# A graph network's two scattering passes: gather rings of twelve steps, transposed indices, and a Gram sum moved

## The chip, the cores and the metric

One core of a Trainium2 chip runs the whole program. The metric is the device time of one execution in microseconds; lower is better. Two kernels are compared by runs on the same chip.

## The reference, cut to what matters

50,000 nodes with 256 features, 12,500 edges sorted by destination. Two layers follow each other.

```python
h = relu(layernorm(x))                     # layer 0
deg = 1 + count of each node in dst
scaled = (h @ W + b) * rsqrt(deg)
x = x + (segment_sum(scaled[dst], src) + scaled) * rsqrt(deg)
h = relu(layernorm(x))                     # layer 1
up = h @ W_up ; tpw = mlp(edge_attr_16) ; sh = edge_attr_4
msg = segment_sum(tensor_product(up[src], sh, tpw), dst)
A = msg @ W_lin ; B = polynomial(A) ; o = B @ WB + h @ Wsc
x = x + batch_normalised(o)                # over all nodes
```

## The kernel before, in words

The core works in stages. A preparation counts degrees and makes the edge weights (to about 155 us). The node pass p1 follows: 98 groups of 512 nodes (`G`), each loaded to one of eight slots of `big`, gives x1 and writes it to `x1_tab`. Then come two edge passes over 49 steps (`S`) of 256 edges each, two rows of 128. The first pass, e1 (about 710 to 1058 us), gathers rows of `x`, computes layer 0's message and scatters it, added, into `x1_tab`. The second, e2 (1058 to 1406 us), gathers rows of `x1_tab`, forms layer 1's message and scatters it, added, into `msg_tab`. The pass e3 over the ranked destinations and the final node pass p2 end the program.

Each engine has its own program, and they meet through semaphores. `done(eng, sem, s, d)` waits until step s-d has been signalled; `landed(eng, slots, s, d)` waits for the transfers of step s-d. A step function `run(eng, n, skew, body, first=2, unroll=4)` writes the first steps out, loops over blocks of `unroll` steps and writes the rest out. `run_written_out` writes out every step.

What sets the order around the change is the program of POOL (GpSimd), which issues every indirect transfer:

- While p1 runs, `dst_step` gathers 98 columns of node data (line 495). `list_step` then makes 98 small scatters to `list_tab` (line 516), each waiting for the one before to land, with one more node gather between them. `pace` (line 489) ties both to the groups that p1 has finished, three transfers a group.
- In e1, step s gathers step s (two transfers, `gather`, line 529) and then scatters step s-4 (two transfers, `scatter_add`, line 540). In e2 it scatters step s-5. The gathered rows lie in `xg`, a ring of four steps inside `big`; a gather waits until ScalarE has read the step that used its slot (`relu` of s-4).
- `scatter_add` waits for `add` (ScalarE's copy of the merged rows, line 1132), for `sidx` (VectorE's target rows) and for the landing of the scatter one step earlier:

```python
done(pool, sm["add"], s, d)
done(pool, sm["sidx"], s, d)
landed(pool, out_sems, s, d + 1, dmas=2)
```

- VectorE and ScalarE wait for step s-4's scatter before they refill the ring of four that holds the target rows and the merged rows (lines 1517 and 1128).

On TensorE, `spread_own` (line 853) lays the step's 128 indices along the free axis by a product with the identity, so that VectorE (e1, line 1493) or ScalarE (e2, line 1200) can compare each index with each other one; `turn` (line 862) transposes features, `merge` (line 870) adds up rows of equal index. e1 also carries the 49 odd groups of p1: SyncE loads them from `x1_odd` to `big` slots 0 to 3 (line 665) once all of x1 has landed, VectorE takes their moments two steps later, and TensorE adds their Gram products (`add_group`, line 801) four steps later, between `turn` and `spread_own`.

Of the kernel before, what the change touches and what calls it, by code (L numbers as in the profile page):

```python
# [33 lines left out]
XS = 8  # L34
NOWHERE = 1 << 20
# [115 lines left out]
def build(nc, x, src, dst, ea16, ea4, W, b, Wup0, Wup1, M1, M2, M3, M4, Wlin0, Wlin1, Wsc0, Wsc1,  # L151
          Wc0, Wc1, WB0, WB1, gamma0, beta0, gamma1, out):
    with ExitStack() as ctx:
# [138 lines left out]
        bsb = poly[:, 4 * D:8 * D].rearrange("p (s k e) -> p s k e", s=2, k=4)  # L292
        squares = sb("squares", [P, 2, 2, D])
# [131 lines left out]
        def _(pool):  # L425
# [72 lines left out]
            def dst_step(s):  # L498
                pace(s.k)
                of_node_step(0, s.k)  # L500
# [11 lines left out]
            def list_step(s):  # L512
                t = s.k
                pace(T + 2 * t)
# [3 lines left out]
                pace(T + 2 * t + 1)  # L518
# [4 lines left out]
            def gather(got_sems, s, which, table, free):  # L523
# [3 lines left out]
                for i in range(2):  # L527
                    t = 2 * s.k + i
                    pool.indirect_dma_start(xg[:, s.slot(0, 4), i, :], None, table, rows_of(idx3[:, which, t:t + 1])  # L529
                                            ).then_inc(got_sems[s.slot(0, 4)].sem, 16)  # L530
# [41 lines left out]

            pool.wait_ge(pre["cleared"].sem, CLEARED)
            run_written_out(S, 5, e2_step)


            def e3_step(s):
                if s.live() and s.k >= 4:
                    gather(e3_got, s, 0, x1_tab, e3_free)
# [160 lines left out]
        def _(pe):  # L740
# [107 lines left out]
            def spread_own(sm, s):  # L848
# [3 lines left out]
                for i in range(2):  # L852
                    last = mm(spread[s.slot(0, 2)][:, i * P:(i + 1) * P],   # L853
# [952 lines left out]
```

## Time and profile before

| | |
|---|---|
| median of three runs | 2046.6 us (2044.68 to 2050.34) |
| the profiled execution's own time | 2046.1 us |
| its span in the trace | 2043.9 us |
| busy share: TensorE, VectorE, ScalarE, POOL | 85%, 84%, 75%, 58% |
| e1, first gather to last landing | about 710 to 1058 us |
| e2 | about 1058 to 1406 us |

All times in the rows are microseconds from the start of the span, and a mean of one is in nanoseconds. A line `L529` is line 529 of the kernel. In a timeline the brackets at the end tell how long the engine sat idle before the instruction and what ended that; "issue" is time in which it waited for nothing that the profile shows. The program's names in a row are those of the memory that is touched: `xg` and the rows of `big` are both `big`, and most small tiles lie in `o_rows`. The chain of waits is followed backwards from the last instruction, step by step, to what released it. POOL is busy here only while it issues a transfer; the transfer itself goes on beside it.

### The profile page before, as it was taken

To read this page: it belongs to the slowest core of one execution; us is meant where nothing else is said; L and a number is where in the kernel's file an instruction comes from. 1 tells how busy PE (TensorE), PEld (TensorE's weight loads), DVE (VectorE), ACT (ScalarE), POOL (GpSimd) and SP (SyncE) were. 2 spreads that over 40 slices of the span, in tenths; PEclk is the share of its full clock that TensorE was granted. 3 is DMA by queue.
4 is the path that set the end of the run, shared out by engine and by line. 5 is a ranking of instruction groups with operands and counts; after the bars stand their busy time and mean duration, and the time that the engine had idled before them with its cause. 6 is when DMAs were issued, how large, how long until landed. Compare 5 with 4: busy or idle time off the path is not lost.

```text
span 2043.9 us, 53847 instructions
## 1 busy us (share of the span) xinstructions
PE 1728.9 (85%) x14740; PEld 1472.5 (72%) x14740; DVE 1710.5 (84%) x7602; ACT 1536.8 (75%) x3485; POOL 1191.1 (58%) x1166
## 2 busy tenths in 40 slices
PE   4988999999999889888857877775999967778885
PEld 3656888888888767777746666664888857777775
DVE  5777999999999878887838888885888879999885
ACT  3756878878787667877756667664999968889885
POOL 3103754455554567777756777776444229998751
PEclk9999999999999999999979899997999979999998
DMA  4669676666766567777745666667655549999994
GB/s 131 241 237 177 230 245 229 235 237 228 246 231 241 183 161 161 162 155 157 161 80 99 119 122 121 118 116 141 186 177 178 170 158 335 337 341 306 376 363 173
DMA packets 186260, 412.09 MB, mean 202 GB/s; under 512 B 48056, under 2 KB 73788, under 8 KB 186186
## 3 DMA queue, kind: packets, MB, share of 16 engines
q1 hardware_dynamic: 116634, 335.50, 47.3%
q0 software_dynamic: 56448, 74.95, 20.4%
q10 hardware_dynamic: 13104, 0.81, 1.6%
q8 instruction: 28, 0.46, 0.1%
q14 instruction: 46, 0.38, 0.1%
HBM read 207.34 MB, written 206.34 MB: 202 GB/s over the span
## 4 chain that ended last, share of the span: by engine, by line
PE 42%; DVE 13%; issue 12%; DMA 12%; POOL 10%; ACT 8%; SPq 1%; DVEq 1%; ACTq 0%; POOLq 0%
PE bank L842 16%; PE bank L822 5%; DVE st L1389 4%; DMA big<-in_x_dram,idx 4%; POOL big L529 4%; ACT hb L1126 3%; POOL msg_tab L540 3%; PE bank L983 3%; PE bank L801 3%; PE bank L838 3%; DMA big<-x_tab,idx 2%; DMA out_dram<-x1b 2%; PE bank L973 2%; POOL x_tab L540 2%; PE bank L862 2%
## 5 line engine op out<-in xcount | busy, mean ns | idle before, releaser
L1389 DVE BATCH_NORM_STATS2 st<-big 128x6 f32<-128x256 f32 x882 | 314.5, 412 | 82.3 <-DMA big<-x_tab,idx 64.1
L842 PE MATMUL bank<-o_rows,ht 128*128 128x256 f32 x1568 | 372.1, 379 | 0.0
L842 PEld LDWEIGHTS bank<-o_rows,ht 128*128 128x128 f32 x1568 | 298.7, 191 | 49.1
L822 PE MATMUL bank<-ident,hb 128*128 128x128 f32 x1568 | 210.8, 278 | 86.4 <-ACT hb L1126 69.6
L529 POOL DMA_INDIRECT big<-x_tab,idx x196 | 193.5, 987 | 149.4 <-issue 139.8
L495 POOL DMA_INDIRECT o_rows<-node_tab,idx x196 | 188.3, 961 | 137.9 <-issue 55.1
L822 PEld LDWEIGHTS bank<-ident,hb 128*128 128x128 f32 x1568 | 177.3, 142 | 116.4 <-issue 88.9
L1126 ACT ACTIVATE hb<-big,rs 128x256 f32<-128x256 f32 x392 | 216.4, 592 | 10.8 <-DVE rs L1412 10.1
L1087 ACT ACTIVATE hb<-big,rs 128x256 f32<-128x256 f32 x392 | 207.4, 590 | 21.2 <-DVE rs L1412 21.2
L1070 ACT ACTIVATE sd<-mv,eps_col 128x4 f32<-128x4 f32 (+1 forms) x343 | 101.0, 295 | 161.8 <-DVE mv L1398 160.4
L1025 PE MATMUL bank<-fin_w,ht 128*128 128x128 f32 x1568 | 203.3, 276 | 0.0
L1025 PEld LDWEIGHTS bank<-fin_w,ht 128*128 128x128 f32 x1568 | 192.1, 193 | 2.3
L540 POOL DMA_INDIRECT x_tab<-o_rows,sidx x98 | 156.1, 1593 | 59.4 <-ACT o_rows L1132 24.9
L1398 DVE BATCH_NORM_AGGREGATE mv<-st 128x2 f32<-128x6 f32 x1470 | 147.2, 158 | 49.4 <-DVE st L1389 7.5
L540 POOL DMA_INDIRECT msg_tab<-o_rows,sidx x98 | 157.2, 1604 | 53.5 <-issue 26.6
L516 POOL DMA_INDIRECT list_tab<-idx,rank_i x98 | 96.7, 987 | 155.7 <-DMA list_tab<-idx,rank_i 126.4
L1469 DVE SCALAR_TENSOR_TENSOR x1b<-bank,o_rows,big 128x192 f32<-128x192 f32 x392 | 183.7, 469 | 0.0
L853 PE MATMUL bank<-ident,own 128*128 128x128 f32 x392 | 74.2, 315 | 98.9 <-DVE own L1533 95.4
L1098 ACT COPY ht<-bank 128x512 f32<-128x512 f32 x196 | 105.3, 589 | 63.3 <-PE bank L822 63.3
L1421 DVE BATCH_NORM_STATS2 st<-big 128x6 f32<-128x256 f32 x392 | 142.8, 407 | 3.3 <-issue 3.3
L1126 ACT ACTIVATE h<-big,rs 128x256 f32<-128x256 f32 x196 | 108.2, 608 | 44.7 <-DVE rs L1412 44.7
L801 PE MATMUL bank<-o_rows 128*64 128x64 f32 (+1 forms) x3136 | 112.9, 224 | 34.2 <-ACT o_rows L1076 34.2
(267 smaller groups left out, 4486.7 us busy)
## 6 DMA issues: line engine op xcount, KB each, us to landing
big<-in_x_dram SPq DMA_DIRECT2D x97, 512.0 KB, 4.2
x_tab<-x1b SPq DMA_DIRECT2D x97, 512.0 KB
big<-x_tab SPq DMA_DIRECT2D x97, 512.0 KB, 5.8
out_dram<-x1b SPq DMA_DIRECT2D x97, 512.0 KB, 4.3
x_odd<-x1b SPq DMA_DIRECT2D x48, 512.0 KB
big<-x_odd SPq DMA_DIRECT2D x48, 512.0 KB
msg_tab<-zeros SPq DMA_DIRECT2D x50, 256.0 KB, 2.2
tpw_tab<-o_rows SPq DMA_DIRECT2D x49, 256.0 KB, 2.0
```

Of the source, the lines that this page charges most:

```text
L495: pool.indirect_dma_start(node_edge[:, t, i, :], None, node_tab, rows_of(idx3[:, i + 1, t:t + 1])).then_inc(node_in[0].sem, 16)
L529: pool.indirect_dma_start(xg[:, s.slot(0, 4), i, :], None, table, rows_of(idx3[:, which, t:t + 1])).then_inc(got_sems[s.slot(0, 4)].sem, 16)
L540: pool.indirect_dma_start(table, rows_of(sidx[:, s.slot(d, 4), i:i + 1]), addb[:, s.slot(d, 4), i, :], None, compute_op=ALU.add).then_inc( ...
L801: return mm(gram[half:half + C, 0:b.shape[-1]], a, b, start=False, stop=False)
L822: last = nc.tensor.transpose(bank[q][:, (2 * j + k) * P:(2 * j + k + 1) * P], hb[:, s.slot(2, 2), 2 * q + j, k * P:(k + 1) * P], ident[:])
L842: last = mm(y, ht[:, q, (2 * j + k) * P:(2 * j + k + 1) * P], w_sb[:, k, :], start=False, stop=(j == 1 and k == 1))
L1025: last = mm(y, ht[:, 2 * s.slot(3, 2) + q, at], fin_w[:, k, :], start=False, stop=(j == 1 and k == 1))
L1087: return s_act(hb[:, a, j, :], xj(big, s.slot(1, XS), D)[:, j, :], ACT.Relu, bias=rs[:, 0, a, 1, j:j + 1], scale=rs[:, 0, a, 0, j:j + 1])
L1126: return s_act(h, row, ACT.Relu, bias=r[:, 1, j:j + 1], scale=r[:, 0, j:j + 1])
L1389: last = v.bn_stats(st[:, k, j, :], row)
L1398: last = v.bn_aggr(mv[:, k, a, j, :], st[:, k, j, :])
L1469: last = v.scalar_tensor_tensor(out=x1[:, j, C:D].rearrange("p (x c) -> p x c", x=3), in0=y[:, C:D].rearrange("p (x c) -> p x c", x=3), sc ...
```

## The change

The ring of gathered steps becomes twelve deep in both passes. In e1 four steps lie in `f_x` and eight in `big` slots 4 to 7; in e2 eight lie in `big` slots 0 to 3 and four in `f_x`. POOL gathers twelve steps before e1's first scatter (ten before e2's, and one more in step 0) and spreads the remaining ones over the steps by `rows_ahead`. It scatters step s in its step s, so `d` is 0. `dst_step` is tied to four transfers a group instead of three, and the tie of `list_step` begins at group 24 instead of 32 and ends at 88 instead of 97. The loops of VectorE and ScalarE over e1 and e2 have blocks of twelve steps. `spread_own` uses transposes. `add_group` in e1 moves to the end of TensorE's step. e3's first four gathers go into e2's last four steps.

```diff
+RING = 12
@@ build
+        head_rows, tail_rows = (big[:, i:i + 4, :].rearrange("p b (h a d) -> p (b h) a d", h=2, a=2) for i in (0, 4))
+        e1_rows = [f_x[:, i] for i in range(4)] + [tail_rows[:, i] for i in range(8)]
+        e2_rows = [head_rows[:, i] for i in range(8)] + [f_x[:, i] for i in range(4)]
@@ POOL
-            def pace(n):
-                if n % 3 == 0 and n // 3 > 3:
-                    pool.wait_ge(p1["x1"].sem, 2 * (n // 3 - 3))
+            def pace(group):
+                if group > 3:
+                    pool.wait_ge(p1["x1"].sem, 2 * (group - 3))
             def dst_step(s):
-                pace(s.k)
+                if s.k % 4 == 0:
+                    pace(s.k // 4)
             def list_step(s):
-                pace(T + 2 * t)
+                if t % 3 == 0:
+                    pace(T // 4 + 2 * t // 3)
...
-                pace(T + 2 * t + 1)
                 of_node_step(1, t)
...
+            def rows_ahead(k, first, last):
+                return [n for n in range(first, S) if (n - first) * (S - last) // (S - first) == k]
+            def e1_gather(k):
+                s = Step(0, k, k, S, 4)
+                gather(e1_got, s, 1, x, lambda s: done(pool, e1["relu"], s, RING), e1_rows[k % RING])
+            for k in range(4):
+                e1_gather(k)
+            for k in range(4, RING):
+                if k % 2 == 0:
+                    pool.wait_ge(p1["x1"].sem, 2 * (G - 4 + (k - 4) // 2))
+                e1_gather(k)
             def e1_step(s):
-                if s.live():
-                    gather(e1_got, s, 1, x, lambda s: done(pool, e1["relu"], s, 4))
-                if s.k == 4:
+                for k in rows_ahead(s.k, RING, 5):
+                    e1_gather(k)
+                if s.k == 0:
                     x1_landed(pool)
-                scatter_add(e1, e1_out, s, 4, x1_tab)
-            pool.wait_ge(p1["x1"].sem, 2 * (G - 4))
-            run_written_out(S, 4, e1_step)
+                scatter_add(e1, e1_out, s, 0, x1_tab)
+            run_written_out(S, 0, e1_step)
             all_landed(pool, e1_out, S, dmas=2)
+            for k in range(RING - 2):
+                e2_gather(k)
+            pool.wait_ge(pre["cleared"].sem, CLEARED)
             def e2_step(s):
-                if s.live():
-                    gather(e2_got, s, 2, x1_tab, lambda s: done(pool, e2["relu"], s, 4))
-                scatter_add(e2, e2_out, s, 5, msg_tab)
-                if s.k == S:
-                    pool.wait_ge(e3["relu"].sem, e3["relu"].base)
-                    all_landed(pool, e2_got, S, dmas=2)
+                for k in rows_ahead(s.k, RING - 2, 6):
+                    e2_gather(k)
+                if s.k == S - 5:
                     pool.wait_ge(pre["list_in"].sem, 16)
-                if s.k > S:
-                    k = s.k - S - 1
-                    gather(e3_got, Step(0, k, k, S, 4), 0, x1_tab, e3_free)
+                if s.k >= S - 4:
+                    k = s.k - (S - 4)
+                    gather(e3_got, Step(0, k, k, S, 4), 0, x1_tab, e3_free, xg[:, k])
+                scatter_add(e2, e2_out, s, 0, msg_tab)
@@ TensorE, spread_own
-                    last = mm(spread[s.slot(0, 2)][:, i * P:(i + 1) * P], 
-                              own[:, s.slot(0, 2), i:i + 1].to_broadcast([P, P]), ident[:],
-                              start=True, stop=True)
+                    last = nc.tensor.transpose(spread[s.slot(0, 2)][:, i * P:(i + 1) * P],
+                                               own[:, s.slot(0, 2), i:i + 1].to_broadcast([P, P]), ident[:])
@@ TensorE, e1_step: from behind turn() to the end of the step
                 if s.live(4):
                     done(pe, odd["relu2"], s, 4)
                     settle(pe)
                     add_group(h2b[:, (s.slot(4, 2) + S) % 2])
@@ ScalarE and VectorE, e1 and e2 (skews as before)
-            run(act, S, 3, e1_step)
+            run(act, S, 3, e1_step, first=1, unroll=RING)
-            run(dve, S, 3, e1_step)
+            run(dve, S, 3, e1_step, first=1, unroll=RING)
```

Where ScalarE's `relu` and VectorE's `edge_moments` read `xg[:, s.slot(.., 4)]` they now read `e1_rows` or `e2_rows` at slot modulo twelve. `gather`'s own wait, that the gather four steps earlier has landed, stays.

## Rows read from the trace of the kernel before

**Rows 1.** The page, its busy time by engine (us, share, instructions).
```profile
PE 1728.9 (85%) x14740; PEld 1472.5 (72%) x14740; DVE 1710.5 (84%) x7602; ACT 1536.8 (75%) x3485; POOL 1191.1 (58%) x1166
```

**Rows 2.** Busy time in stretches; columns: stretch, us, engines, TensorE clock, DMA share, GB/s.
```profile
740.00:1024.00 284.00, 252.38 (x2439) 215.31 (x2440) 227.21 (x1197) 222.19 (x514) 224.66 (x172) 1.00 0.74 159
1089.00:1367.00 278.00, 208.66 (x1678) 178.07 (x1677) 241.97 (x1133) 188.86 (x420) 218.42 (x169) 0.93 0.64 119
```

**Rows 3.** Chain of waits, mid first pass; columns: start, us, what.
```profile
871.35 0.48 ACT o_rows L1132
...
872.10 0.30 POOL x_tab L540
...
874.02 1.57 POOL x_tab L540
...
875.89 1.01 POOL big L529
...
877.21 4.53 DMA big<-in_x_dram,idx
```

**Rows 4.** Timeline of POOL, first pass: first scatter, tail, first gather of second pass.
```profile
733.16 1.63 POOL L540 DMA_INDIRECT x_tab<-o_rows,sidx  x1 [10.57 <-ACT o_rows L1132]
...
1033.96 1.55 POOL L540 DMA_INDIRECT x_tab<-o_rows,sidx  x1 [0.30 <-issue]
1038.51 1.55 POOL L540 DMA_INDIRECT x_tab<-o_rows,sidx  x1 [3.00 <-DMA x_tab<-o_rows,sidx]
...
1057.89 1.02 POOL L529 DMA_INDIRECT big<-x_tab,idx  x1 [3.18 <-DMA x_tab<-o_rows,sidx]
```

**Rows 5.** Chain of waits, end of the second pass.
```profile
1373.49 0.29 POOL msg_tab L540
...
1375.35 3.81 DMA msg_tab<-o_rows,sidx
...
1379.23 0.71 issue
1379.94 2.17 POOL msg_tab L540
```

**Rows 6.** Timeline of POOL, second pass: last early gather, first and last step's scatter.
```profile
1071.75 0.95 POOL L529 DMA_INDIRECT big<-x_tab,idx  x1 [0.30 <-issue]
1082.18 1.61 POOL L540 DMA_INDIRECT msg_tab<-o_rows,sidx  x1 [9.48 <-ACT o_rows L1132]
...
1400.30 1.62 POOL L540 DMA_INDIRECT msg_tab<-o_rows,sidx  x1 [0.57 <-issue]
```

**Rows 7.** Timeline of all engines where the first pass begins.
```profile
711.23 0.29 DVE L1539 COPY o_rows<-o_rows 128x98 f32<-128x98 f32 x1 [1.01 <-DMA o_rows<-node_tab,idx]
...
715.65 16.48 SPq L665 DMA_DIRECT2D big<-x_odd  x5
715.89 0.75 DVE L1389 BATCH_NORM_STATS2 st<-big 128x6 f32<-128x256 f32 x2 [3.70 <-DMA big<-in_x_dram,idx]
...
721.83 1.40 DVE L1389 BATCH_NORM_STATS2 st<-big 128x6 f32<-128x256 f32 x4
```

**Rows 8.** Timeline of POOL while the list is written: first and last list scatter.
```profile
330.97 1.02 POOL L516 DMA_INDIRECT list_tab<-idx,rank_i  x1 [0.42 <-POOL rank_i L509]
...
707.43 0.99 POOL L516 DMA_INDIRECT list_tab<-idx,rank_i  x1 [1.44 <-DMA list_tab<-idx,rank_i]
```

**Rows 9.** Waits by line between 330 and 708; columns: total us, times, longest.
```profile
POOL list_tab L516 <- DMA list_tab<-idx,rank_i: 126.4, 68, 3.9
```

**Rows 10.** Groups of instructions, 740 to 1024: Gram products, spread, turn.
```profile
L801 PE MATMUL bank<-o_rows 128*64 128x64 f32 (+1 forms) x1370 | 49.4, 224 | 31.6 <-ACT o_rows L1076 31.6
...
L853 PE MATMUL bank<-ident,own 128*128 128x128 f32 x168 | 29.9, 300 | 0.0
...
L862 PE MATMUL bank<-ident,o_rows 128*128 128x128 f32 x172 | 25.7, 272 | 0.0
```

**Rows 11.** Waits by line between 740 and 1024.
```profile
DVE rs L1547 <- issue: 3.0, 9, 0.4
```

More of the change, by code:

```diff
@@ L517, in list_step, with gather @@
                                         ).then_inc(list_out[0].sem, 16)
-                pace(T + 2 * t + 1)
                 of_node_step(1, t)
             run_written_out(T, 0, list_step)
-            def gather(got_sems, s, which, table, free):
+            def gather(got_sems, s, which, table, free, rows):
                 landed(pool, got_sems, s, 4, dmas=2)
@@ L528, in gather @@
                     t = 2 * s.k + i
-                    pool.indirect_dma_start(xg[:, s.slot(0, 4), i, :], None, table, rows_of(idx3[:, which, t:t + 1])
+                    pool.indirect_dma_start(rows[:, i, :], None, table, rows_of(idx3[:, which, t:t + 1])
                                             ).then_inc(got_sems[s.slot(0, 4)].sem, 16)
@@ L554, in _, with e2_gather @@
+            run_written_out(S, 0, e1_step)
             all_landed(pool, e1_out, S, dmas=2)
-            def e2_step(s):
-                if s.live():
-                    gather(e2_got, s, 2, x1_tab, lambda s: done(pool, e2["relu"], s, 4))
-                scatter_add(e2, e2_out, s, 5, msg_tab)
-                if s.k == S:
-                    pool.wait_ge(e3["relu"].sem, e3["relu"].base)
-                    all_landed(pool, e2_got, S, dmas=2)
+            def e2_gather(k):
+                s = Step(0, k, k, S, 4)
+                gather(e2_got, s, 2, x1_tab, lambda s: done(pool, e2["relu"], s, RING), e2_rows[k % RING])
@@ L571, in e3_free @@
                 landed(pool, ex_out, s, 4)
-            pool.wait_ge(pre["cleared"].sem, CLEARED)
-            run_written_out(S, 5, e2_step)
+            run_written_out(S, 0, e2_step)
             def e3_step(s):
                 if s.live() and s.k >= 4:
-                    gather(e3_got, s, 0, x1_tab, e3_free)
+                    gather(e3_got, s, 0, x1_tab, e3_free, xg[:, s.slot(0, 4)])
             run_written_out(S, 0, e3_step)
@@ L879, in e1_step @@
                     turn(hg[:, s.slot(2, 2)], bank[0], e1["turned"])
-                if s.live(4):
-                    done(pe, odd["relu2"], s, 4)
-                    settle(pe)
-                    add_group(h2b[:, (s.slot(4, 2) + S) % 2])
                 if s.live():
@@ L900, in e1_step @@
                     last.then_inc(e1["xw"].sem, 1)
+                if s.live(4):
+                    done(pe, odd["relu2"], s, 4)
+                    settle(pe)
+                    add_group(h2b[:, (s.slot(4, 2) + S) % 2])
             run(pe, S, 4, e1_step)
@@ L1160, in e1_step @@
                     for i in range(2):
-                        last = s_act(hg[:, a, i, :], xg[:, s.slot(1, 4), i, 0:D], ACT.Relu,
+                        last = s_act(hg[:, a, i, :], e1_rows[s.slot(1, RING)][:, i, 0:D], ACT.Relu,
                                      bias=rs[:, 0, a, 1, i:i + 1], scale=rs[:, 0, a, 0, i:i + 1])
@@ L1188, in e2_step @@
                     for i in range(2):
-                        last = relu_row(h2[:, a, i, 1:ROW], xg[:, s.slot(1, 4), i, :], rs[:, 0, a], i)
+                        last = relu_row(h2[:, a, i, 1:ROW], e2_rows[s.slot(1, RING)][:, i, :], rs[:, 0, a], i)
                     last.then_inc(e2["relu"].sem, 1)
@@ L1213, in e2_step @@
                     merged_rows(e2, e2_out, s, 4, bank[7])
-            run(act, S, 4, e2_step)
+            run(act, S, 4, e2_step, first=1, unroll=RING)
             def e3_step(s):
@@ L1522, in scatter_to, with edge_moments @@
                 one.end()
-            def edge_moments(sm, got_sems, s, dmas):
+            def edge_moments(sm, got_sems, s, dmas, rows):
                 landed(dve, got_sems, s, 0, dmas=dmas)
-                return moments(sm, "chain_a", 0, [xg[:, s.slot(0, 4), i, 0:D] for i in range(2)], s)
+                return moments(sm, "chain_a", 0, [rows[:, i, 0:D] for i in range(2)], s)
             def take_own(sm, s, index):
@@ L1641, in e2_step @@
                     one.end()
-            run(dve, S, 3, e2_step)
+            run(dve, S, 3, e2_step, first=1, unroll=RING)
             dve.wait_ge(pre["list_in"].sem, 16)
```

6 lines of the change are left out of this document (3 added, 3 removed).

## The prediction

> **What bounds the kernel now.** The page comes first: TensorE and VectorE are busy 85% and 84% of the span and POOL 58% [rows 1]. That is a mean over stages, so the two edge passes, the only stages that the change rebuilds, are read alone. In the middle of e1 POOL is busy 225 of 284 us, VectorE 227, TensorE 252; in e2 218, 242 and 209 of 278 [rows 2]. None is full.
>
> What sets the pace is seen in the starts of POOL's scatters. From e1's first scatter to the gather that waits for all of them lie 324.73 us for 49 steps, 6.63 each [rows 4]; in e2 318.12 us for 48 spacings, 6.63 again [rows 6]. Two stages with unlike arithmetic have one pace. In e1 the chain of waits runs from a gather's landing (4.53 us) over VectorE and ScalarE to the copy of the merged rows, which ends 0.27 us before the scatter that it releases [rows 3]. That is the wait which the deeper ring removes: the gather of step s+1 stands behind the scatter of step s-4 in POOL's program, and the scatter waits for arithmetic that waits for an earlier gather.
>
> A second wait ends almost with it. `scatter_add` waits until the scatter one step earlier has landed. Where e1 has no more gathers, 4.55 us lie between the second scatter of a step and the first of the next, and the releaser is the transfer [rows 4]. At the end of e2 the same: issue to landing 3.81 us, then 0.71 us until the next scatter [rows 5]. With the 1.86 to 1.92 us between a step's two scatters, a step with nothing else on POOL takes 6.41 (1.86 + 4.55) to 6.45 us (1379.94 less 1373.49) [rows 4, 5]. With gathers in between I find 6.58 as the median of e1's 48 spacings and 6.565 of e2's (first and last steps in rows 4 and 6). POOL's own issuing, with two gathers, is 1.92 + 1.87 + 1.32 + 1.25 = 6.36 us [rows 3, 6]. So the serial landing of scatters bounds both passes, POOL's issuing is 0.1 to 0.2 us below it, and the gather's wait that the ring removes is third.
>
> **The change part by part.**
>
> *The ring in the steady passes.* It takes the gather's wait away and 12 of 49 steps' gathers out of e1's loop, so POOL issues (49 x 3.79 + 37 x 2.57) / 49 = 5.7 us a step. The scatter's wait is unchanged, and it is the one left: late next is the landing. What remains to win is the difference between mean and median spacing, which start, end and single late copies make. e1: 49 x 6.58 = 322.4 against 324.7, -2.3 us. e2: 48 x 6.565 = 315.1 against 318.1, -3.0 us. Bounds: nothing at the present pace, and -0.17 x 97 = -16 us if every step falls to the 6.45 of a step without gathers. I take the medians, since three steps in four still carry gathers.
>
> *Ten gathers ahead of e2's first scatter, an eleventh in step 0.* Before, six steps of gathers end at 1072.7 and POOL idles 9.48 us until the first scatter at 1082.18 [rows 6]. Now 22 transfers come first. The first is at 1057.89 [rows 4]; before, the 12th started at 1071.75 and took 0.95 [rows 6]; ten more at 0.95 + 0.30 bring the 22nd to 1084.25, its end to 1085.2 and the scatter to 1085.5: +3.4 us. The arithmetic does not gain from it, since gathers come every 2.5 us either way. e2 in sum: +0.4 us.
>
> *The start of e1.* VectorE is done with p1 at 710.22. It then waits 1.01 us for node data and 3.70 us for the first gather, whose transfers start only when the list is done [rows 7]. The list now starts earlier: the 98 gathers before it, issued at POOL's 1.25 us each, end near 301 where they now reach 331, for the tie of four a group seldom holds. List scatters stay as they are, (707.43 - 330.97) / 97 = 3.88 us each, 126.4 us of it waits for their own landing [rows 8, 9]; that puts the list's end near 683 and the first eight gathers, 10 us, right behind. So both waits go, 4.7 us. VectorE meets the next one two steps later: the odd group's moments at 721.83 would come at 717.1, but SyncE issues that load only at 715.65, when all x1 has landed [rows 7]. A load of 512 KB at the 2 to 4 us in which e1's smaller transfers land [rows 3, 5] arrives at 717.7 to 719.7. I take 718.3, so -3.5 us on e1's first scatter; the ends are 0 and -4.7. Gathers in p1's last 30 us cost nothing: POOL's DMA work is hidden beside compute in p1, and the list work that they displace made as many transfers. If that cover went, p1 would lose at most the 10 us of eight gathers; nothing before points to it.
>
> *Spreading by transpose.* The two products of a step show as four matmul instructions and 29.9 / 43 = 0.70 us; the four transposes of `turn` take 25.7 / 43 = 0.60 us, so two take 0.30 [rows 10]: 0.40 us off TensorE per step. TensorE is busy 252.4 / 43 = 5.9 of 6.6 us in e1, so this is slack beside the scatters: 0. Only in the first steps, before scatters set the pace, can it show, 4 x 0.4 = 1.6 us, twice that at the low clock, over four steps; I take 0, as VectorE is the one without gaps there.
>
> *The Gram sum at the end.* It lets the spread go ahead of a wait for ScalarE; nothing of it stands on the scatter's path and the first live one comes after the first scatter: 0. ScalarE's next `relu2` waits for it a step later, covered by TensorE's 0.7 us of idle time a step; uncovered, it would cost up to its own 49.4 / 43 = 1.15 us a step [rows 10].
>
> *Loops of twelve.* Nine turns of VectorE's loop show 3.0 us, 0.33 each [rows 11]. Three turns are left. Both lie beside the scatters: 0, with at most +-3 us.
>
> *e3's gathers in e2's last steps* sit as before between scatters; e3 starts from the last scatter's landing: 0.
>
> **Sum:** -3.5 - 2.3 + 0.4 = -5.4 us. Against the profiled execution's 2046.1 us (span 2043.9 and 2.2 around it) that gives 2040.7; the median of the runs, 2046.6, is 0.5 higher, so **2041 us**. A measurement of this kernel can tell about 0.3%, 6 us, from no change, and the forecast is just inside.
>
> **Rivals.**
>
> *The ring frees the pass.* If the landing seen in rows 4 and 5 were itself lengthened by the coupled pattern, POOL's issuing or the arithmetic would bound. At 5.97 us a step (POOL's issuing and a small wait) both passes win 98 x 0.66 = 65 us: 1982 us. For it: e1's chain of waits names gathers. Against it: steps without gathers are no faster than 6.41. Chance 0.06.
>
> *The spacing falls to 6.45.* The landing is shorter when gathers are not in step with scatters. At 6.45 the passes win 16 us instead of 5.3: 2030 us; at 6.50, 2035. For it: steps without gathers run so. Chance 0.22.
>
> *The gathers are not early after all.* The list ends with p1, because it is bound by landings and by the groups. The head gains nothing: 2044.5 us. Chance 0.14.
>
> *TensorE's clock falls in e1 (the slower side).* The spread's product is gone and transposes move as little as they do in e2, where the granted clock is 0.93 against e1's 1.00 [rows 2]; TensorE gets more idle time. Work of 5.9 - 0.4 = 5.5 us a step at 2.4 GHz meets the 6.58 us pace until a fifth of it runs at 1.2 GHz, a granted clock of 0.90; from there each hundredth costs 49 x 0.055 x 2 = 5 us, so at 0.88 the kernel stands at 2051 us. For it: e2's clock. Against it: e2's 0.93 leaves its pace at the same 6.63. Chance 0.08. The Trainium skill, TensorE: Matmul & The Clock Gate, section Part 4: PE-mode transpose, says that transposes do not count as busy time for the clock as products do, which speaks against this part of the change; by that rule this rival would be likelier. The transposes of `turn` in e1, as many instructions as the spread's, stand beside a clock of 1.00, so the trace shows no sign of it at this share.
>
> **Numbers.** Forecast 0.50; its own range 2036 to 2046. The second rival reaches down to 2030 and the fourth up to 2051, so 2031 to 2048 leaves out the first, half of the fourth and the end of the second, about 2 in 10 with the unknown costs. Faster by over 0.3% (below 2040.5): the first two rivals and a third of the forecast, 0.06 + 0.22 + 0.16 = 0.44. Slower by over 0.3%: the clock's case, 0.08. Within: 0.48.
>
> **What would show it.** In the changed profile: scatters still 6.5 to 6.6 us apart, now all with the transfer as releaser; VectorE's wait for gathers gone in both passes and a new wait for `add`'s slots, the scatter four steps back, in its place; e1's first scatter near 729.7; e2's first scatter 27.6 us after its first gather; the list done near 683; e1's clock at 1.00. A spacing under 6.3 us would make the reading of the bound wrong; an e1 start before 728 or after 733 the reading of its head.

## The result, and the profile after

The changed kernel takes 2063.64 us (median of five runs, 2057.11 to 2067.74) where the kernel before took 2046.41 beside it: the ratio is 1.0077 with a 95% interval of 1.0054 to 1.0101. The forecast of 2041 us was wrong, and so was its sign. The profiled execution took 2063.85 us with a span of 2062.1, 18.2 us more than the span before.

Four points on POOL's timeline say where the 18.2 us lie: e1's first scatter, e2's first gather, e2's first scatter, and the first scatter of e2's last step. Timeline of POOL, kernel after (start us, duration us, engine, line, operation, idle time before it and what ended it):

```profile
729.62 1.63 POOL L545 DMA_INDIRECT x_tab<-o_rows,sidx  x1 [3.17 <-ACT o_rows L1154]
...
1052.10 1.55 POOL L545 DMA_INDIRECT x_tab<-o_rows,sidx  x1 [3.05 <-DMA x_tab<-o_rows,sidx]
...
1057.91 1.02 POOL L534 DMA_INDIRECT big<-x_tab,idx  x1 [2.41 <-DMA x_tab<-o_rows,sidx]
...
1087.28 1.73 POOL L545 DMA_INDIRECT msg_tab<-o_rows,sidx  x1 [0.30 <-ACT o_rows L1154]
...
1420.91 1.62 POOL L545 DMA_INDIRECT msg_tab<-o_rows,sidx  x1 [0.54 <-issue]
```

| point | before [rows 4, 6] | after | this stretch adds |
|---|---|---|---|
| e1's first scatter | 733.16 | 729.62 | -3.5 |
| e2's first gather | 1057.89 | 1057.91 | +3.6 |
| e2's first scatter | 1082.18 | 1087.28 | +5.1 |
| last step's scatter of e2 | 1400.30 | 1420.91 | +15.5 |
| end of the span | 2043.9 | 2062.1 | -2.4 |

These are the points of one execution of each kernel. The head wins what was forecast, e1 gives it back, and e2 loses 20.6 us: 5.1 before its first scatter and 15.5 in its 48 spacings, which are now 6.95 us in the mean (median 6.92) where they were 6.63 (6.565). e1's median spacing is unchanged (6.58). The -2.4 us of the later stages has no cause in the change that a run shows: from the last step's scatter to the end of the span the twelve kernels of this document take 635.2 to 645.6 us.

The page's busy line and the two windows of the middle of each pass:

```profile
PE 1726.8 (84%) x14544; PEld 1450.5 (70%) x14544; DVE 1699.0 (82%) x7602; ACT 1538.6 (75%) x3485; POOL 1207.0 (59%) x1166
```

```profile
core 0: us, PE busy (x) PEld busy (x) DVE busy (x) ACT busy (x) POOL busy (x), PEclk, DMA share, GB/s
740.00:1024.00 284.00, 254.97 (x2343) 203.85 (x2341) 220.95 (x1194) 222.82 (x513) 205.26 (x154) 0.98 0.72 153
1089.00:1367.00 278.00, 195.25 (x1515) 163.72 (x1513) 227.54 (x1076) 179.95 (x400) 215.00 (x155) 0.90 0.57 111
```

On the page TensorE and VectorE fall by one and two points against [rows 1], POOL rises by one. Against [rows 2] every engine does less in e2's window: VectorE 227.5 us for 242.0, TensorE 195.3 for 208.7. Nobody became the bound by being full; everyone waits more. POOL falls only by 3 us although it starts fewer transfers (155 for 169): its operations became longer. That is the first hint.

**The start of e1** came at the forecast time. SyncE's odd load is issued at 713.26 (715.65 in [rows 7]) and VectorE waits for it:

```profile
713.26 1.79 SPq L688 DMA_DIRECT2D big<-x_odd  x4
```

```profile
718.21 1.40 DVE L1411 BATCH_NORM_STATS2 st<-big 128x6 f32<-128x256 f32 x4 [2.85 <-DMA big<-x_odd]
```

**e1's spacings** are 6.3 to 6.8 us, most of them 6.5 to 6.6, but for three pairs: 8.29 and 7.55 at scatters 2 and 3, 7.30 and 8.51 around the 23rd step, 7.15 and 8.30 around the 35th. The last two pairs lie 12 steps apart, the length of the new loop. Waits by line in e1's window (engine, what waits, what it waits for: total us, times, longest), then VectorE's timeline at the first of the two:

```profile
DVE sidx L1543 <- DMA x_tab<-o_rows,sidx: 17.7, 27, 1.9
...
DVE rs L1569 <- issue: 10.1, 2, 5.2
```

```profile
856.22 0.16 DVE L1543 TENSOR_TENSOR sidx<-sidx_f,trash 128x2 int32<-128x2 f32 x1 [0.48 <-DMA x_tab<-o_rows,sidx]
861.56 0.18 DVE L1569 RECIPROCAL rs<-sd 128x4 f32<-128x4 f32 x1 [5.18 <-issue]
```

At each turn of the loop VectorE does nothing for 5 us and waits for no other engine. In [rows 11] nine turns cost 3.0 us together, none over 0.4. The DMA view shows what goes on meanwhile. Its queue q14 carries instructions, 8192 bytes a packet (queue: packets, MB, share). First the kernel before and the kernel after, both from 740 to 1024; then after again, in the 0.5 us from 859.5, inside the first idle time:

```profile
q14 instruction: 6, 0.05, 0.0%
...
q14 instruction: 21, 0.17, 0.2%
...
q14 instruction: 1, 0.01, 3.9%
```

That packet starts at 859.56 and VectorE works again at 861.56. At every twelve-step turn of the five kernels that have them (after, b_u12, a_late, a_nott and a_psum, four turns each) exactly one instruction packet starts in the idle time, 1.9 to 2.4 us before VectorE goes on. At the nine turns of the four-step loop in the kernel before there is none in the 4 us before.

**e2's spacings.** Groups of the instructions between 1100 and 1400 (busy us, mean ns of one, idle before them by releaser), before and then after:

```profile
L540 POOL DMA_INDIRECT msg_tab<-o_rows,sidx x91 | 145.8, 1603 | 39.7 <-issue 24.8 <-ACT h L1126 8.2 <-ACT o_rows L1132 3.6
```

```profile
L545 POOL DMA_INDIRECT msg_tab<-o_rows,sidx x86 | 149.0, 1733 | 50.6 <-issue 29.1 <-DVE sidx L1543 13.8 <-ACT o_rows L1154 4.5
L1543 DVE TENSOR_TENSOR sidx<-sidx_f,trash 128x2 int32<-128x2 f32 x44 | 7.0, 160 | 47.9 <-DMA msg_tab<-o_rows,sidx 47.9
```

A scatter is issued in 1733 ns instead of 1603. And VectorE, which in this stretch of the kernel before waited 31.5 us for gathers, now waits 47.9 us for scatters to land, since it may write the indices only when the slot's last user is through. One step on the timeline shows what that does. After, POOL and the DVE rows that matter:

```profile
1251.10 1.57 POOL L545 DMA_INDIRECT msg_tab<-o_rows,sidx  x1 [0.31 <-issue]
...
1254.91 0.16 DVE L1543 TENSOR_TENSOR sidx<-sidx_f,trash 128x2 int32<-128x2 f32 x1 [1.00 <-DMA msg_tab<-o_rows,sidx]
...
1255.61 0.55 DVE L1659 TENSOR_TENSOR big<-big,o_rows 128x384 f32<-128x384 f32 x1
1255.71 1.94 POOL L545 DMA_INDIRECT msg_tab<-o_rows,sidx  x1 [0.45 <-issue]
...
1257.95 1.57 POOL L545 DMA_INDIRECT msg_tab<-o_rows,sidx  x1 [0.30 <-issue]
```

The same place in the kernel before:

```profile
1253.73 0.16 DVE L1521 TENSOR_TENSOR sidx<-sidx_f,trash 128x2 int32<-128x2 f32 x1
...
1254.45 0.55 DVE L1637 TENSOR_TENSOR big<-big,o_rows 128x384 f32<-128x384 f32 x1
1255.58 1.62 POOL L540 DMA_INDIRECT msg_tab<-o_rows,sidx  x1 [0.50 <-issue]
```

Before, the addition of the message's vector part (L1637, 128x384, both inputs in SBUF) has ended 0.58 us before the scatter starts. After, the landing releases both VectorE's indices and POOL's next scatter, so the two engines run in step: the same addition (now L1659) starts 0.10 us ahead of the step's first scatter, and that scatter takes 1.94 us instead of 1.62. So it is, 0.02 to 0.10 us ahead, in 30 of the 43 steps between 1100 and 1400. The 0.32 us come on top of the chain "scatter, scatter, landing, scatter" that sets the pace. In 30 steps they are 9.6 us, and over all 49 steps of e2 the first scatter lasts 1.84 us in the mean where it lasted 1.63, 10.4 us in sum. The rest of the 15.5 us is not read from durations: it lies in single longer spacings, two of them at the loop's turns. The theory is therefore: **two prices that the prediction had at nothing, the turn of a twelve-step loop and the new phase of VectorE against POOL's scatters**. The rivals are that the ring's gathers disturb the landings, that ten steps gathered ahead are the loss, and that TensorE's new parts (spread by transposes, late Gram, lower clock) are.

### The profile page after: what moved, and what is told of

It is laid out like the page before. It is cut to its first block, busy times and chain, and to the rows that moved or that the text cites. A ratio compares the mean times of both kernels' runs of the same rounds, so it can differ in the third digit from the quotient of the medians.

```text
span 2062.1 us, 53155 instructions
## 1 busy us (share of the span) xinstructions
PE 1726.8 (84%) x14544; PEld 1450.5 (70%) x14544; DVE 1699.0 (82%) x7602; ACT 1538.6 (75%) x3485; POOL 1207.0 (59%) x1166
## 4 chain that ended last, share of the span: by engine, by line
PE 42%; issue 14%; DVE 13%; POOL 12%; DMA 9%; ACT 8%; SPq 1%; DVEq 1%; ACTq 0%; POOLq 0%
PE bank L865 16%; DVE st L1411 5%; PE bank L845 5%; POOL msg_tab L545 4%; ACT hb L1148 3%; DMA x_tab<-o_rows,sidx 3%; POOL big L534 3%; PE bank L861 3%; PE bank L1005 3%; DMA out_dram<-x1b 3%; PE bank L824 2%; POOL x_tab L545 2%; PE bank L995 2%; PE bank L1009 2%; DMA msg_tab<-o_rows,sidx 2%
## 5 line engine op out<-in xcount | busy, mean ns | idle before, releaser
L1411 DVE BATCH_NORM_STATS2 st<-big 128x6 f32<-128x256 f32 x816 | 289.0, 409 | 32.5 <-DMA big<-x_tab,idx 29.7
L534 POOL DMA_INDIRECT big<-x_tab,idx x164 | 164.7, 1004 | 139.4 <-issue 129.9
L545 POOL DMA_INDIRECT msg_tab<-o_rows,sidx x98 | 169.0, 1724 | 54.9 <-issue 33.1
L1420 DVE BATCH_NORM_AGGREGATE mv<-st 128x2 f32<-128x6 f32 x1470 | 146.9, 158 | 46.1 <-DVE st L1411 10.1
L876 PE MATMUL bank<-ident,own 128*128 128x128 f32 x196 | 44.9, 314 | 144.8 <-DVE own L1555 142.5
L1120 ACT COPY ht<-bank 128x512 f32<-128x512 f32 x196 | 105.4, 589 | 64.4 <-PE bank L845 64.4
L1443 DVE BATCH_NORM_STATS2 st<-big 128x6 f32<-128x256 f32 x392 | 142.9, 407 | 3.3 <-issue 3.2
L632 POOL DMA_INDIRECT out_dram<-o_rows,idx x98 | 96.2, 982 | 77.5 <-SPq L748 50.4
L1297 ACT COPY ht<-bank 128x512 f32<-128x512 f32 x196 | 113.3, 578 | 30.9 <-PE bank L845 30.6
```

What stands on the lines that cost most here:

```text
L534: pool.indirect_dma_start(rows[:, i, :], None, table, rows_of(idx3[:, which, t:t + 1])).then_inc(got_sems[s.slot(0, 4)].sem, 16)
L545: pool.indirect_dma_start(table, rows_of(sidx[:, s.slot(d, 4), i:i + 1]), addb[:, s.slot(d, 4), i, :], None, compute_op=ALU.add).then_inc( ...
L1411: last = v.bn_stats(st[:, k, j, :], row)
L1420: last = v.bn_aggr(mv[:, k, a, j, :], st[:, k, j, :])
L1443: last = v.bn_stats(st[:, 0, j, :], xj(big, s.slot(0, XS), D)[:, j, :])
```

## The experiments

First scatters, spacings and medians below are read from POOL's timeline of each kernel, as those above were. The columns on e1 and e2 are from one execution of each kernel. Where no ratio is given, there is one execution in all, and its profile decides rather than its time. Each ratio is against the kernel before beside it, whose median was 2042.2 to 2046.4 us; medians of different rows differ by that much without any change.

| kernel | median us | ratio to before (95%) | e1 mean | e2: gather to scatter | e2 mean | e2 median |
|---|---|---|---|---|---|---|
| before | 2046.4 | 1 | 6.63 | 24.3 | 6.63 | 6.565 |
| after | 2063.6 | 1.0077 (1.0054 to 1.0101) | 6.72 | 29.4 | 6.95 | 6.92 |
| a_flat | 2064.1 | 1.0077 (1.0050 to 1.0103) | 6.62 | 28.0 | 7.07 | 7.09 |
| a_late | 2051.2 | 1.0022 (0.9988 to 1.0057) | 6.74 | 29.5 | 6.68 | 6.575 |
| a_nott | 2052.1 | one run | 6.70 | 28.7 | 6.71 | 6.595 |
| a_psum | 2058.2 | one run | 6.78 | 29.3 | 6.72 | 6.625 |
| b_u12 | 2060.6 | 1.0081 (1.0047 to 1.0114) | 6.80 | 24.3 | 6.75 | 6.62 |
| b_pe | 2038.9 | 0.9972 (0.9946 to 0.9997) | 6.64 | 24.3 | 6.60 | 6.56 |
| a_flat_late | 2040.6 | 0.9975 (0.9947 to 1.0002) | 6.61 | 28.1 | 6.62 | 6.57 |
| a_fl_p8 | 2037.7 | 0.9970 (0.9944 to 0.9996) | 6.64 | 24.5 | 6.63 | 6.56 |
| a_nope | 2038.1 | 0.9979 (0.9954 to 1.0004) | 6.69 | 24.9 | 6.63 | 6.56 |
| a_two | 2020.1 | one run | 6.60 | 24.8 | 6.33 | 6.415 |

### a_flat: the changed kernel with no loop to turn

VectorE's and ScalarE's loops of both passes are written out in full.

```diff
-            run(dve, S, 3, e1_step, first=1, unroll=RING)
+            run_written_out(S, 3, e1_step, unroll=RING)
```

The other three such calls are changed alike.

> The changed kernel with VectorE's and ScalarE's programs of both edge passes written out, no loop. Theory: the turns of the twelve-step loops stop VectorE (two idle times of 5.2 us each in e1, put down to nothing but issue), and that is what makes six of e1's scatter spacings 7.2 to 8.5 us: without loops the four around scatters 23 and 35 go to 6.6, e1 gets about 7 us shorter, e2 hardly changes (its median spacing of 6.92 is not at the turns); about 2055 us. Rival: the loops cost nothing on the path and the long spacings come from the odd groups' loads or from the clock: 2063 us, spacings as they were.

The forecast of 2055 us was missed. In e1 the theory holds: the 10.1 us of idle time at the turns fall to 0.2, the long spacings around 23 and 35 are gone, and from e1's first scatter to e2's first gather lie 1052.73 - 729.09 = 323.6 us, where after has 1057.91 - 729.62 = 328.3: 4.7 us less (7 were expected). But the kernel is no faster, because e2's spacing rises to 7.07. Timeline of POOL, a_flat, one step of e2:

```profile
1251.23 1.73 POOL L545 DMA_INDIRECT msg_tab<-o_rows,sidx  x1 [0.30 <-issue]
1253.26 1.72 POOL L545 DMA_INDIRECT msg_tab<-o_rows,sidx  x1 [0.30 <-issue]
1255.28 1.50 POOL L534 DMA_INDIRECT f_x<-x_tab,idx  x1 [0.30 <-issue]
1257.09 0.97 POOL L534 DMA_INDIRECT f_x<-x_tab,idx  x1 [0.30 <-issue]
1258.37 1.62 POOL L545 DMA_INDIRECT msg_tab<-o_rows,sidx  x1 [0.31 <-issue]
```

POOL has no gap but the 0.30 us between any two of its instructions: 1.73 + 1.72 + 1.50 + 0.97 + 4 x 0.30 = 7.12 us, the whole step. Here VectorE stands elsewhere in the step. Its message addition starts 0.32 us ahead of the first scatter (1250.91, 1.73 us for the scatter), and another instruction of 128x384 with two SBUF inputs, the multiplication of L1649, starts 0.06 us behind the start of the first gather (1255.34), which takes 1.50 us instead of 1.02. What adds 0.15 us to the second scatter was not tested by a run of its own. In 39 steps of a_flat the product and sum of L1524, 128x256 from SBUF and 0.41 us long, starts 0.1 us ahead of that scatter, which then takes 1.73 us in the mean; in the three steps where it starts 0.3 us ahead, 1.57. POOL's own issuing, the second of the prediction's limits, has become the bound. Removing one loss thus moved the phase into a worse one; alone it would have looked like no effect.

### a_late: the changed kernel with the phase moved

In e2 VectorE writes the scatter's indices (the instruction that waits for the landing) behind the message arithmetic instead of ahead of its last part.

```diff
-                if s.live(2):
-                    scatter_to(e2, last_ones, e2_out, s, 2, 1)
                 if message:
...
                     one.end()
+                if s.live(2):
+                    scatter_to(e2, last_ones, e2_out, s, 2, 1)
```

> The changed kernel with VectorE's e2 step writing the target rows (sidx, and its wait for the scatter four steps back) behind the message's arithmetic instead of between its parts. Theory: a scatter lasts 1.94 us instead of 1.62 because the landing that releases it also releases VectorE, whose 128x384 addition of two SBUF tiles then falls on it in every step; with the wait moved, the addition is over before: the step's first scatter back to 1.6, e2's median spacing 6.92 to 6.6, about 15 us less, 2048 us. Rival: longer scatters come from what lies in the ring (rows in f_x, more gathers in the queue), not from VectorE: spacing stays 6.9, 2063 us.

Group in e2, a_late:

```profile
L545 POOL DMA_INDIRECT msg_tab<-o_rows,sidx x90 | 144.2, 1603 | 51.6 <-issue 23.1 <-DVE sidx L1543 9.6 <-DMA msg_tab<-o_rows,sidx 8.6
```

The addition now starts 2.1 us ahead of the scatter, the scatter's mean is back at 1603 ns, the median spacing at 6.575, and the ratio falls from 1.0077 to 1.0022, 11 us. The two intervals just touch, but the slowest of the ten executions (2056.16 us) is faster than the fastest of the changed kernel's five (2057.11). Same work, same ring, same prefill: only the order on VectorE differs. From e2's first scatter to its last step's lie 320.6 us instead of 333.6, so the phase costs 13.0 of the 15.5 us. The other 2.5 us are still there in a_late, whose turns in e2 take 3.8 and 4.1 us, and gone in a_flat_late (317.5 us), which has no turns.

### a_nott: the changed kernel without the addition

The addition is left out, so the vector part of each message lacks a term.

```diff
-                    v.tensor_tensor(m[:, :, 1:4, :], m[:, :, 1:4, :], outer[:], ALU.add)
```

> The changed kernel without the 128x384 addition of the outer product to the message (line 1659 left out, so the output's vector part lacks a term). Theory: that instruction is what lengthens the scatter: first scatter of a step 1.6 instead of 1.94 us, spacing near 6.6. Rival: another instruction of the same stretch or the ring does it: 1.9 us and 6.9 stay.

Scatters 1603 ns, median spacing 6.595, and e2's 48 spacings take 322.0 us. Taking the one instruction away gives nearly as much as moving it, so it is this addition and not the order as such.

### a_psum: the addition kept, its second input from PSUM

The addition stays in its place with its shape; only where its second operand lies is changed (the vector parts of the messages are not the reference's).

```diff
-                    v.tensor_tensor(m[:, :, 1:4, :], m[:, :, 1:4, :], outer[:], ALU.add)
+                    v.tensor_tensor(m[:, :, 1:4, :], m[:, :, 1:4, :], up[:, :, 1:4, :], ALU.add)
```

> The changed kernel whose 128x384 addition (line 1659) takes its second input from the PSUM bank that holds the up projection instead of from the outer product in SBUF (so the message's vector part is wrong). Same place, same size, one SBUF input less. Theory: VectorE's instructions with two SBUF inputs are what holds POOL's scatter up: first scatter of a step back to about 1.6 us, e2's median spacing near 6.6. Rival: the place or the length of the instruction matters and not where it reads: scatter 1.9 us, spacing 6.9.

Timeline, a_psum:

```profile
1259.36 0.54 DVE L1659 TENSOR_TENSOR big<-big,bank 128x384 f32<-128x384 f32 x1
1259.46 1.62 POOL L545 DMA_INDIRECT msg_tab<-o_rows,sidx  x1 [0.41 <-ACT o_rows L1154]
```

The same 0.10 us of distance, the same 0.54 us of work, and the scatter takes 1.62 us. For this addition the overlap alone costs nothing; it takes two inputs from SBUF. The total of this run is high for a reason ahead of e2: e1 held one spacing of 10.6 us, and e2's first gather came at 1060.51, 6.3 us later than in a_nott, which is 6.1 us faster.

### b_u12: the kernel before with loops of twelve

Nothing of the change but the length of the loops' bodies: all four calls get twelve steps to a turn.

```diff
-            run(dve, S, 3, e1_step)
+            run(dve, S, 3, e1_step, first=1, unroll=12)
```

> The kernel before with only the loops of VectorE and ScalarE in e1 and e2 in blocks of twelve steps, first block written out. Theory: each turn stops VectorE about 5 us as in the changed kernel, and since the old kernel has no steps in hand it loses all of it: two turns in each pass, 10 to 20 us slower, 2057 to 2067 us. Rival: the turn costs 0.3 us as with blocks of four: 2046 us.

Waits by line in e1, b_u12:

```profile
DVE rs L1547 <- issue: 6.6, 2, 3.3
```

Four spacings of 8.2 to 9.6 us stand out, two in each pass and twelve steps apart: (9.56 + 9.54 + 8.16 + 8.37) - 4 x 6.6 = 9.2 us. By the medians of its own comparison the kernel loses 15 us (2060.63 against 2045.68). In the profiled execution, the fastest of the ten with 2052.37 us, e1 and e2 are 14 us longer than before and the later stages 8 us shorter. The 5 us of the passes beyond the turns lie in single spacings of 6.9 to 7.5 us and were not accounted for one by one.

### b_pe: the kernel before with TensorE's parts alone

```diff
-                    last = mm(spread[s.slot(0, 2)][:, i * P:(i + 1) * P], 
-                              own[:, s.slot(0, 2), i:i + 1].to_broadcast([P, P]), ident[:],
-                              start=True, stop=True)
+                    last = nc.tensor.transpose(spread[s.slot(0, 2)][:, i * P:(i + 1) * P],
+                                               own[:, s.slot(0, 2), i:i + 1].to_broadcast([P, P]), ident[:])
```

The Gram block moves from the step's start to its end, as in the change.

> The kernel before with TensorE's two parts of the change alone: indices spread by transposes, the odd groups' Gram products at the end of e1's step. Theory: both passes go by the scatters' landings, so TensorE's 0.4 us a step are slack: no difference, within 0.3% of the kernel before. Rival: its clock falls or the Gram's new place delays ScalarE: slower by 10 us or more; or the spread was on the path: 5 us faster.

2038.92 us, ratio 0.9972 with an upper end of 0.9997: no loss, and at most a gain at the edge of what can be measured. The rival of TensorE is out. (The profiled execution was the slowest of twelve, 2052.22 us; the table's columns on e1 and e2 are its.)

### a_flat_late and a_fl_p8: both losses removed, then eight steps ahead instead of ten

```diff
-            for k in range(RING - 2):
+            for k in range(8):
                 e2_gather(k)
```

The list of later gathers starts at 8 too.

> The changed kernel with both mends: loops of VectorE and ScalarE in e1 and e2 written out, and e2's target rows behind the message. Theory (turns of the loop cost e1 about 6 us, the shared phase costs e2 about 15): each mend gives what it gave alone, now that e2 is no longer held by long scatters; e1's mean spacing 6.62, e2's 6.58; 2063.6 - 12.4 - 6 = about 2044 us, the old kernel's time. Rival: written-out code costs e2 again what it saves (as in the run with it alone, where e2's median spacing rose from 6.92 to 7.09): 2051 us.

> The run before with eight steps of gathers ahead of e2's first scatter instead of ten. Theory: POOL's queue of 22 gathers delays the first scatter by some 5 us against the old kernel (29.4 us after the first gather instead of 24.3); with 18 it starts when its rows are ready, 4 us earlier, and the 48 spacings stay: 4 us less than the run before, about 2040 us. Rival: a shallower ring lets the arithmetic wait for gathers later on: no gain or a loss.

With both losses removed the change stands at 2040.62 us, where 2044 was expected, e1 at 6.61 and e2 at 6.62. That this is within half a microsecond of the prediction's 2041 is luck in part: the kernel before, beside it, ran at 2043.18, and the ratio's interval (0.9947 to 1.0002) holds both the forecast gain and none.

Nor is the gain where the prediction had it. The ring was to take 2.3 us off e1 and 3.0 off e2. From e1's first scatter to e2's first gather lie 323.3 us in a_flat_late and 324.5 in a_fl_p8, where before had 324.7; e2's 48 spacings take 317.5 and 318.1, where before had 318.1. So the deeper ring wins at most 1.5 us in e1 and 0.6 in e2. The uneven spacings at e1's start stay (9.77 us at the third scatter of a_flat_late; 8.50, 7.57 and 8.02 at the second to fourth of a_fl_p8).

Eight steps ahead bring e2's first scatter back to 24.5 us behind its first gather. Timeline of POOL, a_fl_p8, the first and last early gather and the scatter:

```profile
1050.35 1.02 POOL L534 DMA_INDIRECT big<-x_tab,idx  x1 [2.50 <-DMA x_tab<-o_rows,sidx]
...
1071.88 0.95 POOL L534 DMA_INDIRECT f_x<-x_tab,idx  x1 [0.30 <-issue]
1074.81 1.62 POOL L545 DMA_INDIRECT msg_tab<-o_rows,sidx  x1 [1.98 <-ACT o_rows L1154]
```

The last early gather ends 1.98 us before the arithmetic is ready, so eight steps fit at no cost. Ten steps put the scatter behind POOL (0.30 us of idle time ahead of 1087.28). By the timelines this is worth 3.6 us (28.1 - 24.5); the two medians differ by 2.9, with intervals that overlap. At 2037.68 us a_fl_p8 is the fastest version with the right output, but b_pe, which needs no ring, has the same ratio within 0.0002.

### a_nope: a_fl_p8 without TensorE's parts

The spread is a product again and the Gram block stands at the step's start.

> The mended kernel with eight steps ahead, with TensorE's two parts undone (product for the spread, Gram sum ahead of it). Theory: TensorE's parts are slack: the same time within 0.3%, about 2038 us, and e1's first scatter at most 2 us later. Rival: TensorE's parts are what made the mended kernel and the run with them alone a little faster than the old one: 2043 us or more.

2038.12 against 2037.68 us: no difference. e1's first scatter comes 2.6 us later, where at most 2 was expected, but the odd load is also issued 0.7 us later in that execution. With the losses gone the TensorE parts are slack in the new kernel as in the old.

### a_two: what the landing hides

a_fl_p8, where odd steps of e2 scatter into a second table that is never read, and a scatter waits for the landing two steps back instead of one. Half of the messages are thus lost; the number of transfers is the same.

```diff
-                    landed(pool, out_sems, s, d + 1, dmas=2)
+                    landed(pool, out_sems, s, d + len(out_sems), dmas=2)
...
-                scatter_add(e2, e2_out, s, 0, msg_tab)
+                scatter_add(e2, e2_out, s, 0, (msg_tab, msg_odd)[s.k % 2])
```

> As the run with eight steps ahead, but e2's odd steps scatter into a table of their own, which is never read (half of the messages are lost), so that a scatter waits for the landing two steps back. Theory: the serial landing is what bounds e2 at 6.6 us; without it the spacing falls to POOL's issuing or the arithmetic, 5.7 to 6.1 us, 25 to 40 us off e2. Rival: POOL's issuing with its waits bounds: spacing stays above 6.4.

Timeline of POOL, a_two:

```profile
1299.35 1.02 POOL L535 DMA_INDIRECT big<-x_tab,idx  x1 [0.31 <-issue]
1300.67 0.97 POOL L535 DMA_INDIRECT big<-x_tab,idx  x1 [0.30 <-issue]
1301.94 1.64 POOL L546 DMA_INDIRECT msg_odd<-o_rows,sidx  x1 [0.30 <-issue]
1303.88 1.58 POOL L546 DMA_INDIRECT msg_odd<-o_rows,sidx  x1 [0.31 <-ACT h L1149]
1305.77 1.02 POOL L535 DMA_INDIRECT big<-x_tab,idx  x1 [0.30 <-issue]
1307.09 0.97 POOL L535 DMA_INDIRECT big<-x_tab,idx  x1 [0.30 <-issue]
1308.37 1.62 POOL L546 DMA_INDIRECT msg_tab<-o_rows,sidx  x1 [0.30 <-DVE sidx L1544]
```

A step with gathers takes 6.41 to 6.43 us (1308.37 - 1301.94), only 0.15 less than with the landing in the way, and POOL has no gap left. Of the four spacings without gathers three take 3.7 to 3.8 us and one 4.5. So the landing was the limit, and POOL's issuing the next one right below it. The expectation of 5.7 to 6.1 us, 25 to 40 us off e2, was missed: the mean is 6.33, and e2's 48 spacings take 303.8 us, 14 less than in a_fl_p8. It had spread the gathers saved over all steps, while 44 of the 48 spacings still carry two (41 of e2's own steps, and e3's at the end). With POOL's issuing as it is, even a perfect ring could win no more than 0.15 us on those.

## Why the prediction was wrong, by its own steps

**The start of e1: right in the wait that it named, right in the number by luck.** Forecast -3.5 us, first scatter near 729.7; it came at 729.62, with the wait moved to the odd load. But two errors cancel in it. The prediction kept the load's issue at 715.65 and let it land after 2.65 us, from "2 to 4 us" in rows 3 and 5; those rows show 4.53 and 3.81. The load was issued 2.4 us earlier, at 713.26, and VectorE started on it 4.95 us later. The earlier issue is not the ring's doing: b_u12, with POOL's old order, has it at 712.98. Its first scatter is at 733.43, 3.8 us behind that of after, which is the better measure of what the early gathers win. Eight other kernels with the ring have the scatter between 725.8 and 729.2, b_pe with the old order at 741.5, where the list ended 10 us later than before; so the sign holds and the size is good to a few us. The list's end was not right in this execution: its last scatter starts at 691.29, not near 683 (669 to 693 in the others), since it is still held by its own landings; the 16 gathers that fit before VectorE needs them (from 693.85) are enough.

**The bound: right, its pace in e2 wrong.** Scatters' landings set 6.58 us a step in e1, and 6.575 in e2 once the phase is moved (a_late); VectorE's wait for gathers goes. In e2 of the changed kernel the pace is 6.92, outside the 6.5 to 6.6 that was to show the reading right. a_two shows the second limit where rows 3 and 6 had put it. That the ring would bring each pass from its mean spacing to its median isn't seen in any run: see a_flat_late.

**"Loops of twelve ... Both lie beside the scatters: 0, with at most +-3 us": failed.** The price of a turn was taken from a four-step body (0.33 us) for one three times as long. It is 5.2 and 4.9 us in e1, 2.6 in e2, and VectorE has no such slack in one step. Each pass turns twice, not three times. a_flat gives 4.7 us back in e1; b_u12 shows the cause in the kernel before. The row of a turn was in the profile; what was missing is that the row holds for a body of that length alone. The Trainium skill, Runtime: NRT & Kernel Launch, section Instruction fetch mechanics, says that a taken branch to a target outside the small window of instructions held makes the engine wait for a fetch. The traces agree: one instruction packet starts in each of the 20 idle times at a twelve-step turn, 1.9 to 2.4 us before VectorE goes on, and none at the nine short turns. Why the idle time is 5 us in one place and 2.6 in another stays open.

**"e2: 48 x 6.565 = 315.1 ... -3.0 us": failed, the largest term.** It measured 333.6 us, 15.5 more than before, of which a_late gives 13.0 to the phase. The prediction took the spacing as a property of the landing and held the durations of POOL's instructions fixed. Removing the wait for gathers does not leave VectorE where it was: it waits for the landing instead, in step with POOL, and an addition with two SBUF inputs falls on the scatter. a_late, a_nott and a_psum show it in three ways. The Trainium skill, SBUF — State Buffer, section Who interferes with whom, says that a VectorE instruction with two SBUF inputs contends with a GpSimd instruction that reads SBUF; 1.94 against 1.62 us, and 1.62 with the input in PSUM, agree. The same section of the Trainium skill infers that such an addition does not hold up the issue of DMAs, since that needs the write side; the scatters here, which are such issues, say otherwise. The measurement decides.

**"Ten gathers ahead ... +3.4 us": right in kind, too small.** It was +5.1. The chain was read rightly (the scatter stands right behind POOL's 22nd transfer), but three early gathers last 1.4 to 1.5 us instead of 0.95, each with VectorE's multiplication of L1649 starting within 0.1 us of it: the same contention. a_fl_p8 takes it back.

**"Spreading by transpose" and "the Gram sum at the end", both 0: right.** b_pe and a_nope. The saving was sized too high: the spread by transposes takes 18.3 / 43 = 0.43 us a step in e1, not 0.30. The rival of the clock: e1's granted clock is 0.98 with both losses and 1.00 in a_fl_p8, which has the transposes too, and e2's 0.90 goes back to 0.93 there. b_pe has 0.90 in e2 as well and keeps before's pace there (6.60), so nothing here shows time lost by it. The rival's own sum was off: with a fifth of the 5.5 us of work at the low level a step takes 6.6 us, and 5.5 / 6.6 is a mean clock of 0.83, not 0.90. The slower side that the prediction named was the wrong mechanism, and with 0.08 it was too cheap: two parts of the change had been costed at nothing on rows that did not show them in their new form.

**The sum, redone:** -3.5 (head) + 3.6 (rest of e1) + 5.1 (prefill) + 15.5 (e2's spacings) - 2.4 (later stages) = +18.3 us, the span's 18.2 by rounded terms. The 15.5 are 13.0 for the phase and 2.5 for the rest. Of the 10.1 us that VectorE stands still in e1, 7.30 + 8.51 + 7.15 + 8.30 - 4 x 6.585 = 4.9 us get through to the scatters.

## What to carry to other kernels

Removing a wait re-times an engine, and its neighbours' instructions keep their durations only if their overlaps stay: look at what the freed engine will run beside, and above all at which event will release it next; if that event also releases the other engine, they will run in lockstep. Price a longer loop body by a turn of that length, not by the row of a short one. When an undo gives nothing (a_flat), look whether the pass that it helped is offset by another before calling the part harmless. And when a repaired version lands on the forecast, check each stage: here the passes gave almost nothing of what the sum had put there.

## What the runs showed of the hardware

- What a VectorE addition or multiplication of 128x384 (both inputs in SBUF, 0.55 us) does to POOL's issue of an indirect transfer depends on where it starts, from the timelines of e2. Within 0.1 us of the start of POOL's instruction: 1.94 us in the mean for 30 scatters of after (1.62 undisturbed), 1.49 for 34 gathers of a_flat (1.02 undisturbed). Started 0.3 us ahead, it costs a scatter 0.1 us. From 0.3 to 0.5 us behind it: 1.02 for 24 gathers of after; over 1 us behind: 1.55 to 1.62 for the scatters of a_late, but for one that another such instruction met at its start.
- From 0.35 us ahead to 0.1 us behind, the added time is in the mean the end of VectorE's instruction, counted from the start of POOL's, less 0.13 to 0.20 us (scatters and gathers of the traces here alike). That reads as if POOL stood until VectorE was through; it is a reading of durations and was not tested. Between 0.1 and 0.3 us behind both outcomes occur: 2.17 us for the scatter at 1379.94 in [rows 5], 0.17 us after whose start L1627 began, and 1.57 for others. So only the first tenths of the instruction are open to it. With one input in PSUM the addition costs the scatter nothing.
- A turn of a loop costs VectorE 0.33 us with four steps in the body and 2.6 to 5.3 us with twelve (20 turns of five kernels), with the same arithmetic in each step. An 8 KB packet on the instruction queue starts 1.9 to 2.4 us before the end of each of the long idle times.
- With nothing to wait for, POOL leaves 0.30 us between two indirect transfers, in every kernel here; two scatters and two gathers are therefore 1.62 + 1.57 + 1.02 + 0.97 + 4 x 0.30 = 6.38 us of POOL, and a_two, with the landing out of the way, shows 6.41 to 6.43.
